# GpSimd instead of SyncE waits for the last output stores, behind the block of engine programs

## What is computed

```python
x = x + lora_layer(x, cond_8, ...)      # base weights plus 8 mixed low-rank updates
x = x + masked_linear(x, cond_8, ...)   # 8 weights mixed, masked, plus bias
x = x + moe_mlp(x, cond_8, ...)         # softmax, top 2 of 8 gated-gelu experts, plus a shared one
x = x + expert_mlp(x, cond_8, ...)      # argmax picks one gated-silu expert of width 256
```

## Time and profile before

| what | us |
|---|---|
| median of 3 runs | 85.93 |
| lowest and highest of them | 85.29 and 86.2 |
| profiled execution, its time | 85.2 |
| profiled execution, span from first to last instruction of the program | 83.9 |
| difference of these two | 1.3 |

### The profile page before, as it was taken

The page is one execution under the profiler, slowest core; times in us unless marked ns, Lnnn a source line. Parts: engine busy times, 40 slices in busy tenths (PEclk is TensorE's granted clock), DMA queues, the critical chain, the costliest instruction groups (busy, mean ns, idle before and its releaser), DMA issues.

```text
span 83.9 us, 1937 instructions
## 1 busy us (share of the span) xinstructions
PE 81.0 (97%) x620; PEld 77.0 (92%) x620; DVE 48.5 (58%) x115; ACT 31.5 (38%) x59; POOL 15.8 (19%) x20
## 2 busy tenths in 40 slices
PE   6999999999999999999999999999999999999990
PEld 6979988888889989999999999999999999999980
DVE  1489699754337996437438428446465564652271
ACT  6500996865558301122121221221302402316560
POOL 3020577589666600000000000000000000000000
DMA  1997000899990000985869899889899889805202
GB/s 21 334 392 279 2 0 0 240 413 390 420 388 35 0 0 15 308 272 182 314 220 323 238 324 331 277 264 309 268 368 336 311 308 311 331 19 120 99 0 66
DMA packets 5336, 18.51 MB, mean 221 GB/s; under 512 B 592, under 2 KB 1744, under 8 KB 5328
## 3 DMA queue, kind: packets, MB, share of 16 engines
q1 hardware_dynamic: 5040, 17.62, 61.1%
q10 hardware_dynamic: 288, 0.79, 2.4%
HBM read 17.88 MB, written 0.52 MB: 219 GB/s over the span
## 4 chain that ended last, share of the span: by engine, by line
PE 97%; DVE 0%; issue 0%; DVEq 0%
PE bank L690 34%; PE bank L700 17%; PE bank L713 9%; PE bank L727 5%; PE bank L662 4%; PE bank L654 4%; PE bank L670 4%; PE bank L586 3%; PE bank L592 3%; PE bank L622 2%; PE bank L677 2%; PE bank L678 2%; PE bank L680 2%; PE bank L610 2%; PE bank L601 2%; DVE out_sb L507 0%
## 5 line engine op out<-in xcount | busy, mean ns | idle before, releaser
L690 PE MATMUL bank<-x_t,pair_w 128*128 128x128 f32 (+1 forms) x256 | 31.0, 275 | 0.0
L690 PEld LDWEIGHTS bank<-x_t,pair_w 128*128 128x128 f32 x256 | 29.9, 192 | 0.1
L301 ACT ACTIVATE gelu<-bank 128x512 f32<-128x512 f32 x24 | 14.2, 598 | 31.6 <-PE bank L690 27.8
L478 DVE SCALAR_TENSOR_TENSOR hid<-gelu,wsel,bank 128x512 f32<-128x512 f32 x16 | 12.0, 748 | 18.5 <-PE bank L690 18.5
L700 PE MATMUL bank<-hid,pair_w 128*128 128x128 f32 x128 | 16.9, 275 | 0.0
L700 PEld LDWEIGHTS bank<-hid,pair_w 128*128 128x128 f32 x128 | 15.6, 192 | 0.1
L265 POOL TENSOR_TENSOR hid_l<-hid,hid_h 128x512 fp32r<-128x512 f32 x8 | 10.2, 1284 | 4.2 <-ACT hid_h L329 4.2
L476 DVE TENSOR_TENSOR hid<-gelu,bank 128x512 f32<-128x512 f32 x8 | 5.5, 688 | 6.1 <-ACT gelu L301 3.6
L713 PE MATMUL bank<-x_t,w 128*128 128x128 f32 x64 | 8.5, 276 | 0.0
L713 PEld LDWEIGHTS bank<-x_t,w 128*128 128x128 f32 x64 | 7.8, 192 | 0.0
L305 ACT ACTIVATE tanh<-half 128x256 f32<-128x256 f32 x6 | 2.5, 417 | 10.0 <-DVE half L514 10.0
(11 more groups left out here) (70 smaller groups left out, 76.4 us busy)
## 6 DMA issues: line engine op xcount, KB each, us to landing
pair_w<-in_skill SPq DMA_DIRECT2D x16, 768.0 KB, 5.5
w<-in_layer SPq DMA_DIRECT2D x8, 384.0 KB, 5.2
rest_sb<-in_rest SPq DMA_DIRECT2D x1, 661.0 KB, 3.9
x_t<-in_x SPq DMA_DIRECT2D x1, 512.0 KB, 5.4
shared_sb<-in_shared ACTq DMA_DIRECT2D x1, 512.0 KB, 5.2
out_x<-out_sb SPq DMA_DIRECT2D x8, 64.0 KB, 4.1
shared_sb<-in_shared ACTq DMA_DIRECT2D x1, 256.0 KB, 5.4
head_sb<-in_head SPq DMA_DIRECT2D x1, 164.0 KB, 2.3
```

What stands on the lines that cost most here:

```text
L301: act.activation(gelu[:, n, :], ps[:, :], ACT.Gelu_apprx_tanh).then_inc(gelu_ready, 1)
L478: dve.scalar_tensor_tensor(hid[:, n, :], gelu[:, n, :], wsel[:, bass.DynSlice(weight, 1)], u_ps[n][:, :], ALU.mult, ALU.mult).then_inc(hid ...
L690: mm = pe.matmul(ps[:, S * t:S * (t + 1)], pair_w[:, slot, n, 128 * t:128 * (t + 1)], x2_t[:, columns(b)], start=True, stop=True)
```

## The change

The same two waits on the same semaphores with the same values are issued on GpSimd, at the same place behind the block. SyncE's last instruction is now its release from the meeting at the end of the block. Nothing else in the program differs.

```diff
-        def stores_landed(sp):
+        def stores_landed(pool):
 
             for q in range(2):
-                sp.wait_ge(stored[q], 16 * (B // 2))
+                pool.wait_ge(stored[q], 16 * (B // 2))
...
-        stores_landed(nc.sync)
+        stores_landed(nc.gpsimd)
```

## The result

| what | before | after |
|---|---|---|
| median of 22 runs, us | 85.65 | 86.25 |
| lowest and highest, us | 84.89, 86.83 | 85.5, 86.92 |
| profiled execution: time, span, difference | 85.2, 83.9, 1.3 | 85.81, 83.9, 1.9 |

The ratio is 1.0074, with a 95% interval of 1.005 to 1.0099: the changed kernel is slower by 0.4 to 0.85 us. That is within the 1% called "same" above, and clear of zero because there are 22 runs of each.

The account below looks back on a forecast made before the run. TensorE bounds the kernel up to the last product, then the last store's landing. Block 0, landing 0, wait 0, drain 0.2 and two handovers 0.2 sum to +0.4 us on 85.93, giving 86.3 us; range 85.5 to 87.1.

Parts of the forecast that it names:

- Block, landing: Inside the block and at the last store's landing: no instruction added, removed or moved, so cost 0 for each.
- The wait on GpSimd: Behind the block: GpSimd reaches the wait before the landing and ends it as SyncE did; 0, bounds 0 to +0.1 us.
- The drain term: Behind the last instruction: GpSimd's DRAIN at the start takes 188 ns, SyncE's 7 ns; +0.18 us, entered as 0.2.
- Two handovers: At the end: with GpSimd late, word passes between it and SyncE there and back, 0.1 us each way; +0.2 us.
- Time less span: Sign in the changed kernel's profile: the execution's time less its span should grow from 1.3 to about 1.7 us.
- Rival A: Behind GpSimd's last instruction: a long step, hidden before, is exposed; slower from 0.86 us, taken as +1.1, 87.0 us; chance 0.21.
- The other signs: Changed profile: span 83.9 us, L179 under GpSimd with about 28 ns, last store landing about 1.6 us after issue.
- Rival B: Behind SyncE's last instruction: its own share is the long one and becomes covered; faster by 0.8, 85.1 us; chance 0.06.
- Rival C: At the end: landing plus a tail that doesn't ask which engine came last; time stays 85.9 us; chance 0.15.
- The estimate that the prediction made from that page: Closing barrier: another last engine shifts the time by at most about 355 ns, 8 serpentine hops of 44 ns.

## Why the prediction was right

The forecast was 86.3 us, +0.4; measured were 86.25 and a shift of 0.60 (0.56 in the tail). That the time itself is met to 0.05 us is luck. The +0.4 stood on the median of three runs, 85.93, and over 22 runs the kernel before has 85.65; a start 0.28 too high hid a shift 0.2 too small. What was right is the place and the direction: the engines' steps behind the last instruction, with GpSimd's longer and laid open by the change. By its steps:

- *Block, landing.* Predicted at 0. The engines' instructions are the same, and the spans are as before.
- *The wait on GpSimd.* Predicted at 0, bounds 0 to +0.1. From the landing to the end of the wait's instruction it is 67 ns on GpSimd and 44 on SyncE, +0.02. The 0.14 us behind the one landing of the earlier trace rows was therefore no measure of how late GpSimd sees one.
- *The drain term, +0.18.* The direction and the place were right: GpSimd has a longer step of its own than SyncE. The size was short. Measured are 0.54 against 0.12 us, +0.42. The DRAIN at the start of the program was the nearest row, but nothing shows it to be the same step. It also wasn't read quite rightly ("with nothing queued 188 ns is all that is seen"): four memsets of GpSimd surround its start, and the last of them, below, ends at 0.43, when the DRAIN (0.29 to 0.48) is nearly over. So 0.14 of its 188 ns passed while GpSimd was still computing, and no run shows a term of 0.18 us between the two engines' exits.

```profile
0.33 0.10 POOL L828 MEMSET const-uint8-127<- 128x1 uint8 x1
```

- *Two handovers, +0.2.* There is a chain of handovers, and GpSimd sits ahead of SyncE in it. Measured is 0.29 - 0.16 = +0.13, of which 0.07 are the two hops from GpSimd to SyncE and 0.06 a slower step behind SyncE (from update 5 to 6 it is 0.04 us in the kernel before, the one trace with SyncE late, and 0.10 to 0.11 in the nine others). The two terms add to 0.55 where 0.4 was said, and the drain term is the one that was mis-sized.
- *Time less span from 1.3 to about 1.7.* It went to 1.9, between the forecast's value and A's 2.2, and nearer to the forecast's.
- *The other signs.* The span stayed at 83.9 and L179 stands under GpSimd, as said. The record is 43 ns long where about 28 was said, and the last store took 1.8 us where about 1.6 was said, as it did with ScalarE waiting.

Rival A had the right mechanism (a step that was covered and no longer is) with too high a price: the excess is 0.42, half of the 0.86 from which it decides. Rival B is out: SyncE's own share is 0.12 us, and covering it gained nothing that the tails show. Rival C is out, because the tail does ask which engine came last. The serpentine that the Trainium skill describes ("Runtime: NRT & Kernel Launch", "The ~15µs preamble/postamble breakdown"), with 44 ns a hop and 355 ns in all for the barrier ahead of the program, fits the records: in the trace with TensorE late, where nothing holds the chain up once it has begun, the eight hops are 0.36 us in all, but each takes between 0.02 and 0.11. The estimate that the prediction made from that page for another last engine, at most 0.36 us, falls short of the 0.56 measured with GpSimd, since it counted hops and no engine's own step.

## What to carry to other kernels

Time beyond the last instruction belongs to the kernel too. Where an execution's time and its span are both listed, subtract them run by run: the means of ten tails told 0.1 us apart here, while the total strays by more than 1 us. The rest of this paragraph rests on one program, and another may have other steps. Let the engine with the shortest exit be the last to finish, SyncE here, and release GpSimd at least 0.55 us before the end. A final wait on GpSimd, or a meeting of all engines behind the last landing, exposes its exit for 0.5 us and more.

## What the runs showed of the hardware

Behind its last instruction in this program each engine needs a time of its own before it takes part in the closing chain: SyncE 0.12, ScalarE 0.13, VectorE 0.15, TensorE 0.20 us, from one trace each, and GpSimd 0.51 to 0.57, from eight. The chain goes TensorE, ScalarE, GpSimd, VectorE, SyncE and then, as I read the last four updates, back, and the way that is left behind the late engine costs 0.16 (SyncE) to 0.36 us (TensorE). Behind it come the sweep over the semaphores and a second chain: from the ninth update at 84.16 to the last one at 85.31, 1.15 us in the kernel before, and from 84.77 to 85.92, the same 1.15 us, in the changed one. In seven of the other eight traces it is 1.15 to 1.16 us as well, so it hardly depends on who was late; in ScalarE's it is 1.19, in one execution, and why is open. What GpSimd's step is made of stays open: the runs show where it starts, how long it is and what covers it, but not what it does.
